# First feed-forward of a gated cross-attention stack: quantised rows turned back two steps behind instead of one, and ScalarE's first copy moved ahead of the centre operation

## The reference, cut to what matters

```python
def act_quant(x):
    scale = 127.0 / clip(max(abs(x), axis=-1), 1e-05)
    return clip(round(x * scale), -128, 127) / scale

h = bit_linear(layernorm(x), w1)        # 256 -> 1024, both quantised
h = depthwise_conv1d(h, conv_w, conv_b) # 3 taps along the tokens
h = silu(h)
y = bit_linear(h, w2)                   # 1024 -> 256, each row of h quantised by its own largest value
x = x + tanh(g_ffn[0]) * y
```

## Time and profile before

| | |
|---|---|
| median of 3 runs | 1917.15 us (1917.0 to 1918.5) |
| the profiled execution's own time | 1919.29 us |
| its span in the trace | 1917.6 us |
| TensorE busy, over the span | 1650.0 us (86%) |
| VectorE busy | 1160.5 us (61%) |
| ScalarE busy | 882.6 us (46%) |
| the changed stage's loop, first to last L372 start | 195.4 to 412.4 us |
| last second product (L414) starts | 453.2 us |

### The profile page before, as it was taken

The page is one execution under the profiler, slowest core; times in us unless marked ns, Lnnn a source line. Parts: engine busy times, 40 slices in busy tenths (PEclk is TensorE's granted clock), DMA queues, the critical chain, the costliest instruction groups (busy, mean ns, idle before and its releaser), DMA issues. The chain is left out here.

```text
span 1917.6 us, 29587 instructions
## 1 busy us (share of the span) xinstructions
PE 1650.0 (86%) x10149; PEld 1250.2 (65%) x10149; DVE 1160.5 (61%) x2579; ACT 882.6 (46%) x1795; POOL 321.8 (17%) x359
## 2 busy tenths in 40 slices
PE   7797789887899898799997489999936999979998
PEld 5454345556676665688885289999935888854446
DVE  4668567676456566889886823222257898842116
ACT  2332577764532221466653355555544666533213
POOL 0000000000000001211100345555562111001110
PEclk9898899998899999999998689999977999979999
DMA  6000000003000000100004812222261000010002
GB/s 200 1 1 1 1 1 1 1 1 126 1 1 1 1 1 1 31 2 1 2 1 162 322 59 72 73 73 70 72 198 28 1 2 1 2 47 0 0 1 89
DMA packets 62849, 78.83 MB, mean 41 GB/s; under 512 B 13179, under 2 KB 52655, under 8 KB 62319
## 3 DMA queue, kind: packets, MB, share of 16 engines
q1 hardware_dynamic: 42967, 47.35, 7.4%
q0 software_dynamic: 7584, 20.72, 3.4%
q10 hardware_dynamic: 12152, 8.85, 1.5%
HBM read 58.16 MB, written 18.74 MB: 40 GB/s over the span
## 5 line engine op out<-in xcount | busy, mean ns | idle before, releaser
L3003 PEld LDWEIGHTS moe_bank<-moe_xt,moe_w1e 128*128 128x128 f32 x1264 | 155.0, 194 | 5.8 <-DVE moe_xt L2851 1.8
L3003 PE MATMUL moe_bank<-moe_xt,moe_w1e 128*128 128x128 f32 x1264 | 155.8, 277 | 1.1 <-DVE moe_xt L2851 1.1
L3013 PE MATMUL moe_bank<-moe_w,moe_xin 128*128 x632 | 149.3, 379 | 0.0
L3077 ACT ACTIVATE moe_xin<-moe_bank,moe_b 128x128 f32<-128x128 f32 x316 | 90.3, 368 | 125.0 <-PE moe_bank L3003 124.9
L372 PE MATMUL l0f_hb<-l0f_xt,f_w 128*128 128x512 f32 x256 | 125.8, 623 | 5.3 <-DVE l0f_a L306 3.8
L1472 POOL TENSOR_TENSOR all_x<-all_x,l1x_fbias 128x256 f32<-128x256 f32 x32 | 23.4, 735 | 597.6 <-DVE l1x_fxn L204 597.6
L3013 PEld LDWEIGHTS moe_bank<-moe_w,moe_xin 128*128 128x128 f32 x632 | 114.0, 190 | 12.3
L209 DVE BATCH_NORM_STATS2 all_stats<-all_x 128x6 f32<-128x256 f32 x256 | 104.0, 421 | 5.2
L2860 DVE TENSOR_TENSOR moe_y<-moe_bank,moe_b2r 128x256 f32<-128x256 f32 x79 | 33.5, 425 | 118.7 <-PE moe_bank L3013 118.7
L2920 POOL DMA_INDIRECT moe_results<-moe_y,moe_row x79 | 78.0, 988 | 125.1 <-DVE moe_y L2860 121.8
L2851 DVE COPY moe_xt<-moe_bank 128x256 f32<-128x256 f32 x79 | 33.6, 425 | 106.6 <-PE moe_bank L2991 106.6
(11 more groups left out here) (484 smaller groups left out, 3812.7 us busy)
## 6 DMA issues: line engine op xcount, KB each, us to landing
moe_w<-in_L_ffn_W SPq DMA_DIRECT2D x32, 512.0 KB, 10.5
moe_w<-moe_results SPq DMA_DIRECT2D x16, 512.0 KB, 8.7
all_x<-in_x SPq DMA_DIRECT2D x4, 1024.0 KB, 12.6
out_x<-all_x SPq DMA_DIRECT2D x8, 512.0 KB, 2.9
f_w<-in_L_ffn_w_T SPq DMA_DIRECT2D x2, 1024.0 KB, 13.1
moe_inputs<-moe_xin ACTq DMA_DIRECT2D x8, 256.0 KB, 7.2
moe_inputs<-moe_w1e ACTq DMA_DIRECT2D x8, 256.0 KB, 7.8
moe_b2r<-in_L_ffn_b SPq DMA_DIRECT2D x1, 2048.0 KB, 14.1
```

The source lines that it names most:

```text
L3003: ins = nc.tensor.matmul(out, w1e[:, at:at + P], xt[:, u, c * P:(c + 1) * P], start=(c == 0), stop=(c == DC - 1))
L3013: ins = nc.tensor.matmul(bank[4 + u][:, 0:D], ht[:, u, c * P:(c + 1) * P], w2[:, ds(e * (HC * D) + c * D, D)], start=(c == 0), stop=(c == ...
L3077: ins = nc.scalar.activation(ht[:, u, m * P:(m + 1) * P], bank[1 + u][:, m * P:(m + 1) * P], ACT.Gelu, bias=b1[:, ds(e * HC + m, 1)])
```

## The change

The loop gains a step. `turn_back`, the copies and the second product work on tile `t-2` instead of `t-1`, and the update of `x` on `t-3` instead of `t-2`. `zq` gets a second buffer, so `quantise(t)` waits for the turning back of `t-2` instead of `t-1`. On ScalarE the first half's copy stands at the head of the step, ahead of `quantise_x` and `centre`; the second half's stays behind `centre`. PSUM banks are as before.

```diff
-        zq = s.sb("zq", [P, 2, HM * P])
+        zq = s.sb("zq", [P, 2, 2, HM * P])
...
-                for g in range(END + 3):
+                for g in range(END + 4):
...
-                    if 0 <= t - 2 < T:
-                        update(t - 2)
+                    if 0 <= t - 3 < T:
+                        update(t - 3)
...
-                for g in range(END + 2):
+                for g in range(END + 3):
...
-                    if 0 <= t - 1 < T:
-                        turn_back(t - 1, 0, fed)
+                    if 0 <= t - 2 < T:
+                        turn_back(t - 2, 0, fed)
...
-                    if 0 <= t - 1 < T:
-                        turn_back(t - 1, 1, fed)
+                    if 0 <= t - 2 < T:
+                        turn_back(t - 2, 1, fed)
...
-                        turn_x(fed, max(0, 2 * t))
+                        turn_x(fed, max(0, 2 * (t - 1)))
                         fed += 2
-                    if 0 <= t - 1 < T:
-                        down(t - 1)
+                    if 0 <= t - 2 < T:
+                        down(t - 2)
...
                 def quantise(t, half):
                     act.wait_ge(s.sc2_ready, t + 1)
-                    if t:
-                        act.wait_ge(s.back_ps, 2 * (t - 1) + half + 1)
+                    if t >= 2:
+                        act.wait_ge(s.back_ps, 2 * (t - 2) + half + 1)
...
-                for g in range(END + 2):
+                for g in range(END + 3):
                     t = g - LAG
                     b, m = g // M, g % M
+                    if 0 <= t - 2 < T:
+                        copy_q(t - 2, 0)
                     if b < B - 1 and m >= HM:
                         quantise_x((b + 1) * TB + 2 * (m - HM))
                         quantise_x((b + 1) * TB + 2 * (m - HM) + 1)
                     if 1 <= g <= SLOTS:
                         centre(g - 1)
-                    if 0 <= t - 1 < T:
-                        copy_q(t - 1, 0)
-                        copy_q(t - 1, 1)
+                    if 0 <= t - 2 < T:
+                        copy_q(t - 2, 1)
```

More of the change, by code:

```diff
@@ L344, in _ @@
                             input_scales(b + 1)
-                    if 0 <= t - 2 < T:
-                        stats(t - 2)
+                    if 0 <= t - 3 < T:
+                        stats(t - 3)
                     if g == 2:
@@ L401, in turn_back @@
                     for i in range(HM):
-                        ins = nc.tensor.transpose(back_bank(t, half)[:, i * P:(i + 1) * P], zq[:, half, i * P:(i + 1) * P], sh.ident[:, :])
+                        ins = nc.tensor.transpose(back_bank(t, half)[:, i * P:(i + 1) * P], zq[:, t % 2, half, i * P:(i + 1) * P], sh.ident[:, :])
                     ins.then_inc(s.back_ps, 1)
@@ L480, in quantise @@
                     act.wait_ge(s.sc2_ready, t + 1)
-                    if t:
-                        act.wait_ge(s.back_ps, 2 * (t - 1) + half + 1)
-                    nc.scalar.activation(zq[:, half, :], z_bank(t)[:, half * HM * P:(half + 1) * HM * P], ACT.Copy, bias=MAGIC,
+                    if t >= 2:
+                        act.wait_ge(s.back_ps, 2 * (t - 2) + half + 1)
+                    nc.scalar.activation(zq[:, t % 2, half, :], z_bank(t)[:, half * HM * P:(half + 1) * HM * P], ACT.Copy, bias=MAGIC,
                                          scale=sc2[:, t:t + 1]).then_inc(s.zq_ready, 1)
```

## The result

The changed kernel takes 1938.78 us (median of 4 runs, 1938.78 to 1940.38) against 1917.43 us before in the same series (4 runs, 1917.0 to 1918.5): a ratio of 1.0111, 95% interval 1.0098 to 1.0124. Slower by 21 us, where 1937.7 was forecast. Its profiled execution took 1938.79 us with a span of 1937.1, against a span of 1917.6 before.

What follows compares the result with a forecast made beforehand. Bound taken as a ScalarE-VectorE ring of 6.54 us per plain step, not TensorE. Terms 5.9 + 11.5 + 0.3 - 0.4 + 2.7 + 0.5 = 20.5 us, on 1917.15: 1937.7 us, 1.1% slower, range 1931 to 1945.

Steps and rivals of the forecast that it cites:

- The ring: Step loop: ScalarE's quantisings and centre, VectorE's taps, maximum and scale set the step; plain steps 6.54 become 7.03 us.
- the 0.19 given back behind the last x-step: In g = 16 and 24, L311's delay behind L306 vanishes as VectorE comes later: 2 x 0.19 = 0.4 us less.
- the long steps' 0.95: Eight steps behind copy_x: ScalarE idles 0.95 us while the moved copy waits for the one bank `back`; 1.44 each, 11.5 us.
- TensorE's removed wait, at nothing: Step loop: TensorE's wait for the fresh zq, 0.25 us in a plain step, is off the ring, so removing it gains nothing.
- The extra step of the tail, 2.7 us: End of the stage: three tiles instead of two turned back and multiplied after the last turning, adding 2.7 us.
- The changeover, 0.5 between 0 and 1.4: From loop to tail: one tile more behind and TensorE idling longer add 0.5 us, between 0 and 1.4.
- The clock rival: TensorE's clock falls in the steps behind copy_x and at the changeover: about 25.4 us added, 1942.6 us; chance 0.16.
- The faster rival: Step loop: TensorE set the pace, so decoupling it with a second zq buffer pays: -12.2 us, 1905 us; chance 0.04.

Runs made afterwards that it cites:

- lag_only: The changed kernel with the first copy put back behind the centre operation, keeping the lag and two zq buffers: 1919.49 us against 1918.11, ratio 1.0008.
- copy_only: The kernel before with only the first copy moved to the head of the step, on tile t-1 with one zq buffer: 1940.83 us against 1918.11.
- copy_after_qx: The changed kernel with the first copy between quantise_x and the centre operation: 1933.37 us against 1918.11, ratio 1.0083.
- early_lag2: The changed kernel's lag and two zq buffers, centre operation issued a step earlier behind the silu, both copies together at the step's head: 1904.99 us against 1917.70.
- fill_tail: The changed kernel with twelve unused matmuls added in g = 32 and 33, where TensorE idles: 1936.36 us against 1918.11, ratio 1.0098.
- the second trace: The kernel before run once more, unchanged, for another trace: 1918.58 us, one run.
- early_lag1: The kernel before with the centre operation of slot g issued in step g, behind the silu of slot g-1: 1918.95 us against 1917.70, ratio 1.0007.

## Why the prediction was right

**The ring.** Right, with its lengths. Plain steps 7.03 forecast, 7.03 to 7.04 measured; behind `copy_x` 9.78 and 9.76 in six of the eight steps, while the two without L456 (g = 16 and 24) went from 7.56 to 8.96, by the same 1.4; g = 12 and 20 longer by 0.15 where 0.16 was said; the 0.19 given back behind the last x-step is there too (6.74 became 7.04, not 7.23). The loop's sum was 17.3 us, its measure 17.1. `lag_only` and `copy_only` show that the move is the cause, and `copy_after_qx` that the long steps' 0.95 is the bank.

**TensorE's removed wait, at nothing.** Right: shown by `lag_only`, which takes it from the first L402 (0.30 us of waiting then stands before the second) and leaves the loop at 214.0 us, and by `early_lag2`, where it begins to count once the ring is cut.

**The extra step of the tail, 2.7 us.** Right: the last two L414 are again 2.74 us apart, and the tail with the clock held is 2.9 us above the first trace of before.

**The changeover, 0.5 between 0 and 1.4.** This is the term that was mis-sized. The tail grew by 5.2 us, so the term measured 2.5, above its upper bound. 2.3 of that is TensorE's clock, by `fill_tail`; what the waits alone add is 0.2. I took the bound from the excess of one L388 and one L414 in the earlier trace rows. In that execution the lower clock cost the path almost nothing: the next L483 starts 4.22 us behind the last L304, against 4.15 in the second trace, where these two groups ran at the upper level. The changed kernel idles for 3.94 us there, and three groups in a row on the path run at the lower level. The size depends on what it is held against: with before's second trace, which met the clock on the path as well, the term is 45.0 - 41.7 - 2.7 = 0.6, inside the bounds. `copy_only` and `early_lag1`, which also turn back one tile behind, have tails of 41.5 and 41.4 us, so the 39.8 from which I worked looks like a lucky execution, though one trace of each kernel does not prove it.

**The clock rival.** Half right. Its first half, L402 slower in the long steps, did not happen: the granted clock is 1.00 from 249 to 434 us, although each long step holds a wait of 1.8 us. Its second half, the changeover, did. The Trainium skill ("TensorE: Matmul & The Clock Gate", section on HAM oscillation) lets waits between bursts of matmuls bring the lower clock. The trace agrees at the changeover (0.67, behind 3.94 us of idling) and not in the long steps; the waits of the page's own case are longer than the 1.8 us here, so that the prediction's "by that rule this rival holds in full" said more than the page does. Nor does the length of the last wait sort the cases in these traces: the clock fell behind 1.55 us in one execution of the kernel before and stayed up behind the same 1.55 us in the other.

**The faster rival.** Wrong for this kernel as it stands, and instructive. The Trainium skill's reading of consistent bubbles ("Perfetto Trace Analysis", optimization strategy) would have had more `zq` buffers pay. `lag_only` has them and gains nothing; `early_lag2` has them on a kernel whose ring is open and is 12.7 us faster than the kernel before. The buffer, with the step of lag that it allows, is worth something only where the wait that it removes is on the ring.

**The total.** 20.5 us forecast, 21.4 measured by the medians. That they differ by only 0.9 is in part luck: the ring was 0.2 too high and the changeover 2.0 too low, while all that lies outside the stage happened to be 2.8 shorter than in the first trace of before. Held against the second trace of before, the stage grew by 20.4 us and the rest by nothing.

**A reading that failed.** I said that TensorE's waits for L483 would vanish and one for L490 appear. The wait appeared, 0.79 us, but the trace goes on naming L483 for it; only the copy's end, 0.10 us ahead, tells.

## What to carry to other kernels

Before moving an instruction, write down the ring that sets the step, with the distance of each link, and see on which side of it the instruction stands: the same 0.49 us copy is free in the part where its engine waits for the ring and costs its full length in the part where the ring waits for its engine. Taking a wait off the busiest engine is worth nothing while another ring is longer, and after cutting one ring look for what the freed instruction itself waits for, since that closes the next. An operation that reads the only bank should not stand directly behind another that reads it; put something between that needs neither.

## What the runs showed of the hardware that was not expected

- Adding twelve useless 128x512 matmuls shortened the stage by 2.3 us: put where TensorE was idle for 2.5 and 3.9 us, they keep it at its upper clock level, and the eight L388 that follow take 1.04 us instead of 1.91.
- One and the same program lost 1.9 us more in one execution than in another at the same place (41.7 against 39.8 us from the last L304 to the barrier), with a granted clock of 0.74 against 0.87 over the 13 us behind that L304.
- The same wait at the same place brings the lower clock in one execution and not in another. Behind 2.51 us of idling in g = 32, L402 takes 0.63 us in both traces of the changed kernel and 1.09 in `copy_after_qx`, whose instructions there are the same; for the kernel before the wait is 1.55 us, with L388 at 1.53 and at 1.04 us. In `early_lag2` the granted clock stayed at 1.00 over the 18 us of the changeover, with waits of 1.67 and 2.16 us.
- The part ahead of the stage is the same code in all kernels, and yet the first L304 came anywhere from 194.3 to 202.1 us in the eleven traces, while the loop behind it repeated to 0.1 us where a kernel was traced twice.
